# A causal attention stage in a new order with silu by tanh, and a rebuilt last stage of experts per token

## The reference, cut to what matters

```
x = x + attention(norm(x), ctx, ctx, mask)                 # one head
x = x + encoder_experts(norm(x))                           # 4 experts, each batch uses its best 2
x = x + causal_attention(norm(x), ctx, ctx)                # 16 heads of 16, the causal stage
x = x + token_experts(norm(x))

def token_experts(x):
    sh = ln(silu(x @ sw1.T + sb1) * (x @ sw2.T + sb2), s_ln_g, s_ln_b)   # shared expert, 128 hidden
    shared_out = sh @ sw3.T + sb3
    x_moe = x[index_b, index_t]                            # 512 tokens
    s, e = sigmoid(x_moe @ sg_w.T + sg_b), sigmoid(x_moe @ eg_w.T + eg_b)
    top = argmax(e + exp_bias)                             # one of 8 experts per token
    w = softmax([s, e[top]])
    z = ln(silu(x_moe @ ew1[top].T + eb1) * (x_moe @ ew2[top].T + eb2), ...)
    expert_out = z @ ew3[top].T + eb3
    return shared_out.at[index_b, index_t].set(shared_out[index_b, index_t] * w[0] + expert_out * w[1])
```

## Time and profile before

| | |
|---|---|
| median of 3 runs | 836.39 us (835.06 to 837.0) |
| the profiled execution | 835.16 us, its span 833.4 us |
| busy, share of the span | PE 87%, DVE 78%, POOL 45%, ACT 40% |
| 105 to 550 us (encoder) | PE 432.86 of 445 us, DVE 354.91 |
| 560 to 719 us (causal stage) | PE 137.28 of 159 us, DVE 148.69, ACT 76.92, POOL 68.41 |
| table loads on ACT | one in the whole span, 1.3 us |
| 740.6 to 833.4 us (last stage) | PE 58.66 of 92.8 us, DVE 56.26, POOL 31.55; granted clock 0.72 |

### The profile page before, as it was taken

The page is one execution under the profiler, slowest core; times in us unless marked ns, Lnnn a source line. Parts: engine busy times, 40 slices in busy tenths (PEclk is TensorE's granted clock), DMA queues, the critical chain, the costliest instruction groups (busy, mean ns, idle before and its releaser), DMA issues.

```text
span 833.4 us, 29134 instructions
## 1 busy us (share of the span) xinstructions
PE 723.0 (87%) x10978; PEld 571.7 (69%) x10978; DVE 650.1 (78%) x1858; ACT 337.4 (40%) x710; POOL 379.1 (45%) x647
## 2 busy tenths in 40 slices
PE   4788469999999999999999999998889888734895
PEld 3567447888888888888888888876556656412673
DVE  4786556787878788887877888789999999845965
ACT  4656224444343444434343444434445545412200
POOL 2788712435353454535444453543345345254132
PEclk9766589999999999999999999999999999955797
DMA  7776300000000000000000000002221222122000
GB/s 272 244 238 226 140 2 2 4 2 4 2 3 3 2 4 3 3 3 3 3 4 3 3 4 9 9 22 73 91 89 60 78 90 80 32 86 75 5 1 6
DMA packets 24655, 41.24 MB, mean 49 GB/s; under 512 B 3727, under 2 KB 16665, under 8 KB 24267
## 3 DMA queue, kind: packets, MB, share of 16 engines
q1 hardware_dynamic: 23096, 37.39, 13.6%
q0 software_dynamic: 704, 1.71, 0.8%
q10 hardware_dynamic: 726, 0.30, 0.1%
HBM read 30.86 MB, written 8.91 MB: 48 GB/s over the span
## 4 chain that ended last, share of the span: by engine, by line
PE 69%; DVE 17%; POOL 5%; issue 5%; ACT 4%; DMA 1%; POOLq 0%; ACTq 0%; DVEq 0%; SPq 0%
PE ps L480 7%; PE ps L474 7%; PE ps L482 6%; PE ps L481 6%; PE ps L684 6%; PE ps L666 5%; DVE mx L1403 5%; PE ps L616 4%; PE ps L722 3%; PE ps L724 3%; PE ps L723 3%; PE ps L618 3%; PE ps L617 3%; PE ps L608 2%; POOL w_lo L1826 2%
## 5 line engine op out<-in xcount | busy, mean ns | idle before, releaser
L1040 ACT ACTIVATE pT<-ps 128x1024 f32<-128x1024 f32 x96 | 93.1, 1022 | 124.5 <-PE ps L666 124.5
L1799 POOL TENSOR_TENSOR rs<-mv,cst 128x1 f32<-128x1 f32 x132 | 31.2, 236 | 178.6 <-DVE mv L1174 140.9
L1403 DVE TENSOR_REDUCE mx<-ps 128x16 f32<-128x2048 f32 x48 | 109.4, 2280 | 1.0 <-PE ps L639 1.0
L1887 POOL TENSOR_TENSOR y<-y,vec 128x256 f32<-128x256 f32 x32 | 23.2, 726 | 170.7 <-DVE y L1177 170.7
L722 PE MATMUL ps<-xh,w_hi 128*128 128x128 bf16 x512 | 99.4, 219 | 0.0
L723 PE MATMUL ps<-xl,w_hi 128*128 128x128 bf16 x512 | 99.3, 219 | 0.0
L724 PE MATMUL ps<-xh,w_lo 128*128 128x128 bf16 x512 | 99.3, 219 | 0.0
L1801 POOL TENSOR_TENSOR rs<-rs,cst 128x1 f32<-128x1 f32 x132 | 73.2, 554 | 10.3
L480 PE MATMUL ps<-w_hi,hh 128*128 x256 | 69.8, 273 | 0.0
L481 PE MATMUL ps<-w_hi,hl 128*128 x256 | 69.8, 273 | 0.0
L482 PE MATMUL ps<-w_lo,hh 128*128 x256 | 69.8, 273 | 0.0
(11 more groups left out here) (366 smaller groups left out, 2495.1 us busy)
## 6 DMA issues: line engine op xcount, KB each, us to landing
stage<-in_w SPq DMA_DIRECT2D x32, 384.0 KB, 3.7
vec<-in_vec SPq DMA_DIRECT2D x4, 896.0 KB, 5.8
vec<-in_tw SPq DMA_DIRECT2D x12, 256.0 KB, 2.8
ctxc<-in_ctx SPq DMA_DIRECT2D x19, 128.0 KB, 2.2
comb<-x SPq DMA_DIRECT2D x16, 128.0 KB, 1.7
comb<-t SPq DMA_DIRECT2D x16, 128.0 KB, 1.8
shared<-x1b SPq DMA_DIRECT2D x16, 128.0 KB, 1.7
out<-x SPq DMA_DIRECT2D x16, 128.0 KB, 1.8
```

The costliest lines, as they stand in the source:

```text
L1040: A(pT[:, 8 * a:8 * a + 8, :].rearrange("p h q -> p (h q)"), ps[:, 2 * a:2 * a + 2, :].rearrange("p g k -> p (g k)"), ACT.Exp, scale=SCALE ...
L1403: nc.vector.tensor_reduce(mx[:, :], att.rearrange("p g s k -> p (g s) k"), AX.X, ALU.max, negate=True).then_inc(m_max, 1)
```

## The change

**Silu.** The shared expert and the token experts use silu(h) = h (1 + tanh(h/2)) / 2. ScalarE computes tanh in place of exp; VectorE needs one fused instruction where it had an addition, a reciprocal and a product. The factor 0.5 goes into the gate's product.

**Order of `block_c`.** On TensorE `scores(m)` comes directly after `projection_v`, ahead of the second half of `values(n)`; then `sh_out`, `sh_transposes`, `o_rows`, `prep`, `shift_transpose`, `o_transposes`, `scores_T`, `sh_first`, `sh_z` and, last, `out_proj`. `scores_T` writes three of its masks before it waits for `mT`. On VectorE `maxima` and `shift_split` follow `qk_low` directly, `o_norm` comes behind them, silu and gate stand just ahead of `x3`, and `sh_zlow` is done for batch b-4 ahead of `bias_v`, where it was done for b-3 near the end. ScalarE is ordered to match. `block_c` runs for b = 1 to 17; what is left of the shared expert for batches 14 and 15 is put between the steps of the last stage.

**Tokens.** The rows and keys per token are made in three pieces after the encoder's blocks 9, 13 and 17. `keys_as_rows` is gone, with two of its DMAs: TensorE spreads the keys over a row with four matmuls into bank 0. `last_of_equal` runs for all four groups before the router. `gather_tokens` moves to `block_c(17)`.

**Experts.** `choice` uses banks 2 and 3. The order is changed on TensorE and VectorE so that a group's hidden products come before the output of the group two earlier; `gated` loses the addition and the reciprocal, and works in `hD`, which lies in `pT`. The gather of the shared rows comes after the first group's z.

```diff
@@ TensorE, scores_T
-                pe.wait_ge(qk_split, u + 1)
-                pe.wait_ge(mT_sb, u + 1)
                 if causal:
-                    for g in range(4):
+                    for g in (1, 2, 3, 0):
+                        if g == 0:
+                            pe.wait_ge(mT_sb, u + 1)
                         mm(ps[:, g, :], identb[:, :], causb[:, 1:2, :].broadcast_to([128, 4, 128]),
                            start=True, stop=False)
@@ TensorE, block_c
                     projection_v(None)
+                    pe.wait_ge(pT_b, n + 1)
+                    scores(m, True)
...
                 if served(b):
                     o_rows(n)
+                if served(b + 2):
+                    pe.wait_ge(qk_split, m + 1)
+                    prep(b + (B + 2), True)
                 if more:
-                    scores(m, True)
+                    shift_transpose(m)
+                if served(b):
+                    o_transposes(n)
+                if more:
+                    scores_T(m, True)
...
-                if served(b):
-                    o_transposes(n)
-                if more:
-                    shift_transpose(m)
                 if served(b - 3):
                     sh_z(b - 3)
                 if served(b):
                     out_proj(n, None)
-                if more:
-                    scores_T(m, True)
@@ TensorE, before and in the last stage
+            pe.wait_ge(d_gidx, 1)
+            pe.wait_ge(pT_b, UNITS + B)
+            for t in range(MT):
+                last = mm(ps[:, 0, 128 * t:128 * t + 128], ids[:, 4, t:t + 1].broadcast_to([128, 128]), ident,
+                          start=True, stop=True)
+            last.then_inc(d_keys, 1)
...
+            sh_out(B - 2, B - 1)
             pe.wait_ge(tg_split, 1)
...
+            sh_z(B - 1)
             pe.wait_ge(d_sel, D1)
...
-            for step, t in ((choice, 0), (choice, 1), (chosen_hidden, 0), (choice, 2), (chosen_hidden, 1), (choice, 3),
-                            (chosen_z, 0), (chosen_hidden, 2), (chosen_out, 0), (chosen_z, 1), (chosen_hidden, 3),
-                            (chosen_out, 1), (chosen_z, 2), (chosen_out, 2), (chosen_z, 3), (chosen_out, 3)):
+            choice(0)
+            choice(1)
+            chosen_hidden(0)
+            sh_out(B - 1, B - 1)
+            for step, t in ((choice, 2), (chosen_hidden, 1), (choice, 3), (chosen_hidden, 2), (chosen_z, 0),
+                            (chosen_hidden, 3), (chosen_z, 1), (chosen_out, 0), (chosen_z, 2), (chosen_out, 1),
+                            (chosen_z, 3), (chosen_out, 2), (chosen_out, 3)):
                 step(t)
@@ ScalarE
-                A(sde[:, 0:HM], h[:, 0:HM], ACT.Exp, scale=-1.0).then_inc(s_e, 1)
+                A(sde[:, 0:HM], h[:, 0:HM], ACT.Tanh, scale=0.5).then_inc(s_e, 1)
@@ VectorE, sh_silu
-                ts(sde[:, HM:2 * HM], sde[:, 0:HM], 1.0, None, ALU.add).then_inc(s_e1, 1)
-                dve.wait_ge(s_e1, b + A1)
-                nc.vector.reciprocal(sde[:, 0:HM], sde[:, HM:2 * HM]).then_inc(s_r, 1)
-                dve.wait_ge(s_r, b + A1)
-                tt(h[:, 2 * HM:3 * HM], h[:, 0:HM], sde[:, 0:HM], ALU.mult).then_inc(s_a, 1)
+                stt(h[:, 2 * HM:3 * HM], sde[:, 0:HM], 1.0, h[:, 0:HM], ALU.add, ALU.mult).then_inc(s_a, 1)
@@ VectorE, block_c
                 if served(b - 3):
                     sh_gnorm(b - 3)
+                if served(b - 4):
+                    sh_zlow(b - 4)
                 if served(b + 1):
                     bias_v(m, 1 - slot, vc[:, VC_V:VC_V + D])
                     qk_low(m)
...
                     maxima(m)
                     shift_split(m)
                 if served(b):
+                    o_norm(n)
+                if n - 2 < UNITS:
+                    sum2(n - 2, slot)
+                if served(b + 2):
+                    y_low(b + (B + 2), 2 * KC)
+                if served(b - 4):
+                    sh_sum(b - 4)
+                if served(b - 1):
+                    sh_low(b - 1)
+                if served(b):
                     o_low(n)
...
+                if served(b - 2):
+                    sh_silu(b - 2)
+                    sh_gate(b - 2)
+                if served(b):
+                    x3(n, b, slot)
...
@@ VectorE, last stage
+            dve.wait_ge(row_in, 16)
+            dve.wait_ge(d_keys, 2)
+            for t in range(MT):
+                last_of_equal(t)
+            sh_zlow(B - 2)
...
+            sh_gnorm(B - 1)
+            sh_sum(B - 2)
...
+            mask_tokens(0)
+            mask_tokens(1)
+            sh_sum(B - 1)
+            stored_rows()
+            for step_of, t in ((mask_tokens, 2), (gated, 0), (gated_norm, 0), (mask_tokens, 3), (gated, 1), (mask_z, 0),
+                               (gated_norm, 1), (gated, 2), (mask_z, 1), (gated_norm, 2), (gated, 3), (mask_z, 2),
+                               (gated_norm, 3), (final, 0), (mask_z, 3), (final, 1), (final, 2), (final, 3)):
                 step_of(t)
```

More of the change, by code:

```diff
@@ L812, in block_c @@
                 if more:
-                    if not isinstance(b, int) or b >= 4:
+                    if b >= 4:
                         pe.wait_ge(s_zsplit, b + (A1 - 4))
@@ L893, in _ @@
             pe.wait_ge(tb_in, 16)
+            pe.wait_ge(tw_lo, TCHUNKS)
+            pe.wait_ge(tw_hi, TCHUNKS)
             def choice(t):
@@ L1112, in block_c @@
                     tw(*weights)
+                if served(b + 2):
+                    prep(b + (B + 2), 2 * KC)
+                if served(b + 1):
+                    shift(m)
                 if served(b):
                     oo(n)
-                if served(b + 1):
-                    shift(m)
-                if served(b - 3):
-                    sh_zhi(b - 3)
-                if served(b + 2):
-                    prep(b + (B + 2), 2 * KC)
-                if served(b - 1):
-                    sh_e(b - 1)
             for n in range(-1, UNITS + 1):
                 block(n, prep_of(n + 2))
-            for b in range(1, B + 4):
+            for b in range(1, B + 2):
                 c = b - LOOP_C
                 block_c(b, (c, c // 2 + 1, c % 2) if 0 <= c < TCHUNKS else None)
+            sh_zhi(B - 2)
             act.wait_ge(tg_in, 16)
@@ L1584, in block_c @@
                 n, m = b + UNITS, b + (UNITS + 1)
-                rest = n if isinstance(n, int) else 2 * UNITS
                 if served(b - 1):
@@ L1602, in block_c @@
                     qk_low(m)
-                if served(b - 4):
-                    sh_sum(b - 4)
-                if served(b):
-                    o_norm(n)
-                if served(b - 1):
-                    if rest - 2 < UNITS:
-                        sum2(rest - 2, slot)
-                    sh_low(b - 1)
-                if served(b - 2):
-                    sh_gate(b - 2)
-                if served(b + 1):
                     maxima(m)
@@ L1633, in _, with i_link, tokens_wrapped, tokens_outside @@
             dve.wait_ge(vec_in, 16 * E)
+            links = [0]
+            def i_link(ins):
+                links[0] += 1
+                ins.then_inc(d_idx, 1)
+                dve.wait_ge(d_idx, links[0])
+            fb, ft, tmp, flat, key = (ids[:, k, :] for k in range(5))
+            def tokens_wrapped():
+                dve.wait_ge(idx_in, 32)
+                for k, f, size in ((0, fb, B), (1, ft, S)):
+                    i_link(cp(f, idx_i[:, k, :]))
+                    i_link(ts(tmp, f, 0.0, float(size), ALU.is_lt, ALU.mult))
+                    i_link(tt(f, f, tmp, ALU.add))
+            def tokens_outside():
+                i_link(ts(tmp, fb, 0.0, None, ALU.is_lt))
+                i_link(ts(flat, fb, float(B - 1), None, ALU.is_gt))
+                i_link(tt(tmp, tmp, flat, ALU.add))
+                i_link(ts(flat, ft, 0.0, None, ALU.is_lt))
+                i_link(tt(tmp, tmp, flat, ALU.add))
+                i_link(ts(flat, ft, float(S - 1), None, ALU.is_gt))
+                i_link(tt(tmp, tmp, flat, ALU.add))
+            def tokens_flat():
+                i_link(ts(key, tmp, float(4 * B * S), None, ALU.mult))
+                i_link(ts(fb, fb, 0.0, float(B - 1), ALU.max, ALU.min))
+                i_link(ts(ft, ft, 0.0, float(S - 1), ALU.max, ALU.min))
+                i_link(ts(fb, fb, float(S), None, ALU.mult))
+                i_link(tt(flat, fb, ft, ALU.add))
+                i_link(tt(key, key, flat, ALU.add))
+                i_link(cp(gidx[:, :], flat))
+                nc.vector.memset(junk[:, 2:3], 0.0).then_inc(d_gidx, 1)
+            def last_of_equal(t):
+                i_link(stt(row_tmp, ps[:, 0, :], ids[:, 4, t:t + 1], pos, ALU.is_equal, ALU.mult))
+                i_link(nc.vector.tensor_reduce(ids[:, 5, t:t + 1], row_tmp, AX.X, ALU.max))
+            def stored_rows():
+                i_link(tt(ids[:, 6, :], ids[:, 5, :], cst[:, C_M:C_M + MT], ALU.is_gt))
```

(7 more changed lines are left out.)

145 lines of the change are left out of this document (52 added, 93 removed).

## The result

The change makes the kernel slower, as forecast: 847.52 us (median of 4 runs, 846.37 to 848.54) against 835.72 for the kernel before on the same chip, ratio 1.014 with an interval of 1.0116 to 1.0164. The forecast was 844. The profiled execution has a span of 844.7 us against 833.4. Five pieces of the span make up the 11.3 us. Each runs from one start of `maxima` to another (there are 48 in a run), or to an end of the span. "`maxima` of batch b" is the one issued in `block_c(b)`, as in the earlier trace rows; that of batch 14 is the last of the run.

A forecast was written before the change was run, and what follows sets the result against it. The causal stage was taken as bound by a ring of waits between engines. +21.9 ring, +4 clock, +0.3 encoder, -1.2, -2.95, -12.8 and -1.3 after it sum to +8 on 836.39: 844 us, range 818 to 860.

The forecast's parts named there:

- Ring: Causal stage: waits through VectorE, TensorE and GpSimd, from `maxima` to `maxima`, take 14.3 us per batch against 12.26; +21.9 us.
- Batch 1: Causal stage: `maxima` of batch 1 no longer stands behind four instructions and comes at 558.2, 2.2 us sooner.
- The rival with VectorE as the pace: Causal stage: if VectorE still set the pace, a batch would take about 11 us; given no chance of its own.
- Idle time before `x3`: Causal stage: VectorE idles some 1.8 us in each batch, waiting for TensorE's `out_proj`.
- VectorE is done with its own list by 5.65: Causal stage: VectorE finishes its work ahead of `x3` 5.65 us after `maxima` starts, while `x3` comes at 7.48.
- Clock: Causal stage: TensorE's wait of 2.4 to 2.5 us before `projection_v` lowers the granted clock in one batch of four; +4 us.
- The bounds of 0 and 16: Causal stage: limits of the clock loss in us, the upper from 11 waits at 1.5 us each.
- Encoder: Encoder: 21 chained VectorE token instructions in three units, 1.2 to 1.6 us each; bounds 0 and 4.2, taken as +0.3 us.
- Last stage: After the last `maxima`: tokens -1.2, tokens to router -2.95, router to last sum -12.8, last scatter -1.3 us.
- Tanh: ScalarE alternating Exp and Tanh: table loads cost between 0 and 36 us; taken as 0, no load added.
- 1.1 us per batch go: Causal stage, VectorE: silu falls from three instructions to one, leaving about 10.4 us of VectorE work per batch.
- the ring does not close: Causal stage: VectorE's or TensorE's own work decides, some 11.2 us per batch, about 804 us in all; chance 0.14.

The follow-up runs named there:

- e10: Changed kernel with GpSimd making the reciprocal deviation of the shared expert's gated product ahead of the residual stream's; 836.03 us, 1.0008 of the kernel before.
- e1: Changed kernel with the split of the shared expert's z (`sh_zhi`, `sh_zlow`) back one block earlier, as before the change; 846.48 us.
- e11: Changed kernel with the split of z one block earlier and `out_proj` right behind `scores_T`, ahead of `sh_first` and `sh_z`; 823.49 us.
- e2: Changed kernel with the shared expert's silu made as before by Exp, addition, reciprocal and product; 846.75 us.
- e3: Kernel before with only the shared expert's silu changed, to Tanh and two fused products, order and last stage kept; 848.75 us.
- e4: Changed kernel with the causal stage's old order on TensorE, ScalarE and VectorE, tanh, tokens and last stage as changed; 832.43 us.
- e7: Changed kernel with the causal stage's old order, plus 34 unused matmuls on TensorE before its wait for `mtile`, from batch 3 on; 823.86 us.

## Why the prediction was right, point by point

- **Ring.** Forecast 14.3 us per batch, measured 14.09 undisturbed. The four legs agree one by one, in the rows of 647.62 to 661.70: `maxima` to `x3` 7.31 us (forecast 7.48), to `stats_c` 1.42 (1.53), to `projection_v` 3.03 (2.99), to `maxima` 2.32 (2.32); so the number isn't luck. Batch 1 came 2.2 us sooner as said, and batches 1 to 14 took 185.9 us against 183.1 + 4 of clock. That these waits set the pace is shown three times, with the work kept the same: 0.44 us out of GpSimd's part gave 0.54 (e10), `sh_zlow` out of it gave 1.01 (e1), `out_proj` forward gave another 0.46 (e11). The rival with VectorE as the pace is excluded by e2, where 0.4 us more of its work left the interval as it was.
- **Idle time before `x3`**: forecast 1.8, measured 0.87. The step "VectorE is done with its own list by 5.65" left out the port: the gate takes 1.13 us there and ends at 6.44. In this order the idle time hid it.
- **Clock.** Forecast +4, measured 5.5 us in five of 13 intervals, after waits of 1.79 and 2.33 us (forecast for the second: 2.4 to 2.5). The first of these waits, 1.79 us for `mtile`, is one the prediction had no term for. The bounds of 0 and 16 were not too wide: e1 reaches the upper one, with a shorter wait.
- **Encoder.** "+0.3" was wrong: +2.3 us. It was sized by the wait of 1.11 us, but the pieces stand ahead of `norm1`, not in that wait, take 1.7 to 1.9 us each, and one instruction in each takes 0.7 us instead of 0.17 beside one of GpSimd. VectorE, then GpSimd:

```profile
300.03 0.16 DVE L1674 TENSOR_TENSOR ids<-ids 128x4 f32<-128x4 f32 x1
300.22 0.70 DVE L1675 TENSOR_SCALAR ids<-ids 128x4 f32<-128x4 f32 x1
```

```profile
300.18 0.72 POOL L1891 TENSOR_TENSOR ybo<-y,vec 128x256 f32<-128x256 f32 x1
```

- **Last stage.** `maxima` to tokens -1.3 (forecast -1.2), tokens to router -2.8 (-2.95), router to the end of the last sum -11.9 (-12.8), sum to scatter -0.6 (-1.3). Together -16.7 against -18.25; the roughest term, the last, was half of what I took.
- **Tanh.** No table load, as taken. But "1.1 us per batch go" was only half an account. In the new order it gains nothing (e2); in the old one it costs 13.7 us (e3), which the prediction had nowhere.
- **The rival "the ring does not close"**, 11.2 us per batch and 804 us, was priced too low: no kernel of this study gets under 12.10 us, not even with the old order and tanh. That VectorE sets the pace of the kernel before was half the truth; a ring through TensorE is equally long. Its average of 12.26 us per batch also holds the two intervals of 12.77 and 12.76 with the collision (e3).

The net of 11.3 us, where 8 were forecast, is thus the last stage's -16.7, the encoder's +2.3, the early `maxima`'s -2.2, +1.0 at the start, which can't be put down to the change, and +26.9 in the causal stage. Of these 26.9 us, 13.7 come with tanh alone and the old order (e3, e4), and 13.2 more with the new one; but the two don't add as causes, since e2 shows the first without effect once the second is there. The forecast was 3.4 us short: the ring without the clock cost 2.7 us less than forecast, and encoder, clock, last stage and start 6.0 us more, so part of the closeness of 844 to 847.52 comes from errors that cancel. Why the clock falls in one batch and not in the next is not explained.

## What to carry to other kernels

When an order is changed, walk every cycle from one batch's step to the same step of the next, through all engines and queues, before counting any engine's work; a saving counts only if it lies on the longest one, and the second longest is often just behind. When one engine gets ahead, look at what shares its neighbour's port at the new time: here a shorter silu let GpSimd go first, and an added wait on an engine off the ring was worth 16 us. And price idle time in front of TensorE twice, once for itself and once for the clock.

## What the hardware did that I had not expected

- A 128x128 product on VectorE takes 0.28 us alone and 0.99 to 1.13 us when GpSimd's 128x512 instruction started 0.2 to 0.3 us ahead of it, plain (before, at 705.73) or fused (e3, e4, e11). A 128x4 instruction goes from 0.17 to 0.70 us. None of this shows as idle time: the instruction's own duration grows.
- The length of a wait does not decide whether the clock falls. It stood at 0.50 behind waits of 1.79 us (at 590.05 in the changed kernel), of 2.00 us in e1 and twice of 1.12 to 1.14 us in e11 (at 588.01 and 690.56), and at 1.00 behind nine others of 1.12 us there, behind six of the ten waits of 2.33 us in the changed kernel and behind 2.12 us. In e4 it went down and up in turn, behind 2.17 and 2.12 us, but in e3 it fell behind two waits of 2.12 us (at 668.46 and 722.60) and stood behind two of 2.16 (at 601.29 and 614.09). What decides is open.
- 34 matmuls that nothing reads, put into such a wait, made the kernel 1% faster (e7, in the old order; not tried in the new one).
